# Linear attention in a decoder kernel: two row groups and two heads per unit, value blocks as stationary operand

## The reference, cut to what matters

```python
def _L2_attn_ref(x, W_qkv, W_out):
    nH, Hs = (16, 8)
    qkv = (x @ W_qkv.T).reshape(Bx, Tx, 3 * nH, Hs).transpose(0, 2, 1, 3)
    q, k, v = (qkv[:, :nH], qkv[:, nH:2 * nH], qkv[:, 2 * nH:])
    q = jax.nn.softmax(q, axis=-1) * Hs ** (-0.5)
    k_exp = jnp.exp(k - jnp.max(k, axis=2, keepdims=True))
    k_exp_cumsum = jnp.cumsum(k_exp, axis=2)
    kv_cumsum = jnp.cumsum(jnp.einsum('bhtc,bhtd->bhtcd', k_exp, v), axis=2)
    kv = kv_cumsum / (k_exp_cumsum[..., None] + 1e-09)
    xo = jnp.einsum('bhtc,bhtcd->bhtd', q, kv)
    return xo.transpose(0, 2, 1, 3).reshape(Bx, Tx, Dm) @ W_out.T
x = _layernorm(x + _L2_attn_ref(x, L2_attn_W_qkv, L2_attn_W_out), axis=-1)
```

## Time and profile before

| | us |
|---|---|
| median of 3 runs | 2258.78 (2258.63 to 2259.35) |
| profiled execution, its own time | 2261.14 |
| its span, first to last instruction | 2259.4 |
| mean granted TensorE clock in the span | 0.841 of 2.4 GHz |
| TensorE busy (matmul) | 1642.3, 73% |
| VectorE busy | 1300.3, 58% |
| ScalarE busy | 739.4, 33% |
| GpSimd busy | 385.6, 17% |

### The profile page before, as it was taken

The page is one execution under the profiler, slowest core; times in us unless marked ns, Lnnn a source line. Parts: engine busy times, 40 slices in busy tenths (PEclk is TensorE's granted clock), DMA queues, the critical chain, the costliest instruction groups (busy, mean ns, idle before and its releaser), DMA issues. The chain is left out here.

```text
span 2259.4 us, 25576 instructions
## 1 busy us (share of the span) xinstructions
PE 1642.3 (73%) x9160; PEld 1227.4 (54%) x9160; DVE 1300.3 (58%) x2377; ACT 739.4 (33%) x1362; POOL 385.6 (17%) x411
## 2 busy tenths in 40 slices
PE   3788888896759969994735984966835674876595
PEld 2466666675537656662524973655523662653373
DVE  4699999993755551114566546335245936733853
ACT  1456565651214423321211331012303223333242
POOL 0565655551000000000100000000001005001300
PEclk7799999997869989996767996967967976788597
DMA  5011111101000001000001210000010000000000
GB/s 171 26 34 34 35 34 35 34 13 48 1 0 1 1 0 53 31 10 0 1 0 67 101 56 0 1 1 0 1 75 1 1 1 0 1 1 1 0 1 10
DMA packets 21244, 49.79 MB, mean 22 GB/s; under 512 B 4752, under 2 KB 9232, under 8 KB 20880
## 3 DMA queue, kind: packets, MB, share of 16 engines
q1 hardware_dynamic: 21136, 48.40, 6.4%
HBM read 47.29 MB, written 1.10 MB: 21 GB/s over the span
## 5 line engine op out<-in xcount | busy, mean ns | idle before, releaser
L186 POOL TENSOR_TENSOR rstd<-spread,minus_half 128x4 f32<-128x4 f32 x36 | 36.7, 1020 | 1460.9 <-DVE spread L168 1460.9
L906 PE MATMUL l0h_scores<-l0h_k_rot,l0h_q_slots 128*128 128x128 f32 (+1 forms) x1024 | 206.9, 349 | 0.0
L906 PEld LDWEIGHTS l0h_scores<-l0h_k_rot,l0h_q_slots 128*128 128x128 f32 x1024 | 170.0, 208 | 13.1
L1110 POOL TENSOR_TENSOR l0h_k_part<-large_weights,l0h_sines 128x512 f32<-128x512 f32 x64 | 83.2, 1299 | 219.8 <-PE l0h_scores L906 127.1
L986 ACT ACTIVATE l0h_scores<-l0h_scores,l0h_top 128x128 f32<-128x128 f32 (+1 forms) x256 | 100.4, 392 | 26.1 <-DVE l0h_top L1063 26.0
L1485 DVE TENSOR_TENSOR l0e_weighted<-l0e_out_ps,l0f_weight 128x512 f32<-128x512 f32 x18 | 12.5, 692 | 151.0 <-PE l0e_out_ps L1447 151.0
L882 PE MATMUL l0h_projected<-XT,l0h_wq 128*128 128x256 f32 x256 | 71.0, 401 | 18.9 <-DVE l0h_q_rot L1050 9.8
L1467 ACT ACTIVATE l0e_hidden<-l0e_hidden_ps,l0e_experts 128x512 f32<-128x512 f32 x72 | 49.5, 687 | 107.2 <-PE l0e_hidden_ps L1433 107.2
L1444 PE MATMUL l0e_out_ps<-l0e_experts,l0e_hidden 128*128 128x128 f32 x576 | 82.5, 286 | 0.0
L1057 DVE TENSOR_TENSOR l0h_q_slots<-l0h_q_rot,l0h_chosen 128x1024 f32<-128x1024 f32 x64 | 78.4, 1225 | 7.0 <-DVE l0h_q_rot L1054 0.5
L1111 POOL TENSOR_TENSOR l0h_k_rot<-large_weights,l0h_cosines 128x512 f32<-128x512 f32 x64 | 81.9, 1280 | 0.0
(11 more groups left out here) (682 smaller groups left out, 4057.3 us busy)
## 6 DMA issues: line engine op xcount, KB each, us to landing
l1e_experts<-in_l_experts SPq DMA_DIRECT2D x16, 768.0 KB, 4.2
l0h_chosen<-l0h_chosen_dram SPq DMA_DIRECT2D x64, 128.0 KB, 2.9
l0e_experts<-in_l_experts SPq DMA_DIRECT2D x9, 578.0 KB, 3.8
l0h_pos<-l0h_pos_dram SPq DMA_DIRECT2D x64, 64.0 KB, 2.0
small_weights<-in_w_l_ffn SPq DMA_DIRECT2D x1, 4016.0 KB, 13.4
large_weights<-in_w_l_xattn SPq DMA_DIRECT2D x1, 2632.0 KB, 9.2
l0h_wq<-in_l_wq SPq DMA_DIRECT2D x16, 128.0 KB, 2.9
large_weights<-in_w_l_attn SPq DMA_DIRECT2D x2, 512.0 KB, 6.6
```

Of the source, the lines that this page charges most:

```text
L906: mm = nc.tensor.matmul(at[:, slot], q_slots[:, s % 2, slot, part, i * P:(i + 1) * P], k_rot[:, s % 2, part, 0:KEYS[i][1]], start=False, s ...
L1110: nc.gpsimd.tensor_tensor(k_part[:], source, at_batch(sines, s), ALU.mult)
```

## The change

- `flat` gets a block of 32 columns for each tile and head: 24 zeros and then the head's 8 values, and 24 zeros at the very end (4120 columns). The values are copied with gaps, and GpSimd clears 128 runs of 24 columns.
- A unit is now (b, p, jj): the row groups p and p + 2 and the heads 2jj and 2jj + 1 of each. `weigh` has four matmuls with 32 rows and 256 columns, which alternate between the two row groups; the two groups write to different PSUM banks.
- In the products the masked block is the moving operand and 32 columns of `flat` are the stationary one. The window is shifted by 8 columns for each head, so the four heads of a group fill the 32 output partitions 32g to 32g + 31 and are added in PSUM with zeros elsewhere. The result is already turned: features by partitions, tokens by columns.
- The cross part is one matmul for each batch with `state` as stationary operand (L1954 of the new kernel), added to the second tile's columns of the same PSUM bank. The cross product, its copy and the block with the addition are gone.
- ScalarE copies 256 columns for each batch, four times, and `close_sublayer` is called with `features_t`.

```diff
-        flat, values = padded_values(k, "l2a_values", T, HX, DX, ctx)
-        values = values.rearrange("p t h d -> p t (h d)")
-        running, queries, heads_out = sb("running", [P, N]), sb("queries", [P, 4, N]), sb("heads_out", [P, T, P])
+        flat = sb("values", [P, T * HX * 32 + 24])
+        blocks = flat[:, 0:T * HX * 32].rearrange("p (t h e) -> p t h e", t=T, h=HX)
+        values = blocks[:, :, :, 24:32]
+        running, queries, heads_t = sb("running", [P, N]), sb("queries", [P, 4, N]), sb("heads_t", [P, N])
...
-             lambda act, out: nc.scalar.copy(flat[:, 0:N], out)),
+             lambda act, out: nc.scalar.copy(values.rearrange("p t h d -> p (t h) d"),
+                                             out.rearrange("p (a d) -> p a d", d=DX))),
...
-                    nc.gpsimd.memset(flat[:, N:], 0.0)
+                    nc.gpsimd.memset(blocks[:, :, :, 0:24], 0.0)
+                    nc.gpsimd.memset(flat[:, T * HX * 32:], 0.0)
...
-            weights_ps = k.ps("l2a_weights_ps", [P, 2, TB, 4, P], inner)
+            weights_ps = k.ps("l2a_weights_ps", [P, 2, 2, TB, 2, P], inner)
...
-            units = [(b, g) for b in range(B) for g in range(4)]
+            units = [(b, p, jj) for b in range(B) for p in range(2) for jj in range(2)]
...
-                            mm = nc.tensor.matmul(weights_ps[:, n % 2, i], k_t[rows, tile], queries[rows, :, tile],
-                                                  start=True, stop=True)
+                            for o in range(2):
+                                rows = slice(32 * (p + 2 * o), 32 * (p + 2 * o) + 32)
+                                mm = nc.tensor.matmul(weights_ps[:, n % 2, o, i], k_t[rows, tile],
+                                                      queries[rows, 2 * jj:2 * jj + 2, tile], start=True, stop=True)
...
+                        for y in range(2):
+                            j = 2 * jj + y
+                            for i in range(TB):
+                                for o in range(2):
+                                    g = p + 2 * o
+                                    at = ((TB * b + i) * HX + 4 * g + j) * 32 + 24 - 8 * j
+                                    mm = nc.tensor.matmul(out_ps[32 * g:32 * g + 32, b % 2, i * P:(i + 1) * P],
+                                                          flat[:, at:at + 32], weights[:, n % 2, o, i, y, :],
+                                                          start=(j == 0 and i == 0), stop=False, skip_group_check=True)
+                        mm.then_inc(unit_ready, 1)
+                        if n % per_batch == per_batch - 1:
+                            nc.tensor.matmul(out_ps[:, b % 2, P:2 * P], state[:, b, :], q_t[:, b * S + P:(b + 1) * S],
+                                             start=False, stop=True, skip_group_check=True).then_inc(out_ready, 1)
...
-                        for i in range(TB):
-                            for j in range(4):
-                                mm = nc.tensor.matmul(out_ps[:, n % 2, (i * 4 + j) * DX:(i * 4 + j) * DX + P],
-                                                      weights[:, n % 2, i, j, :],
-                                                      flat[:, ((TB * b + i) * HX + 4 * g + j) * DX:][:, 0:P],
-                                                      start=True, stop=True)
-                        mm.then_inc(out_ready, 1)
...
-                second = heads_out[:].rearrange("p (b i) n -> p b i n", i=TB)[:, :, TB - 1, :]
-                nc.vector.tensor_tensor(second, second, cross[:], ALU.add)
-        close_sublayer(k, "l2a_close", heads_out[:], [W("wout")], 1)
+        close_sublayer(k, "l2a_close", None, [W("wout")], 1, features_t=[heads_t[:]])
...
-                pe.wait_ge(state_ready, 1)
-                for b in range(B):
-                    mm = nc.tensor.matmul(cross_ps[:, b, :], q_t[:, b * S + P:(b + 1) * S], state[:, b, :], start=True,
-                                          stop=True)
-                mm.then_inc(cross_ready, 1)
```

More of the change, by code:

```diff
@@ L1921, in weigh @@
                     def weigh(n):
-                        b, g = units[n]
-                        rows = slice(32 * g, 32 * g + 32)
+                        b, p, jj = units[n]
                         if n >= 2:
@@ L1931, in weigh, with product @@
                         mm.then_inc(ready, 1)
+                    def product(n):
+                        b, p, jj = units[n]
+                        pe.wait_ge(masked, n + 1)
+                        if n % per_batch == 0 and b >= 2:
+                            pe.wait_ge(out_used, b - 1)
+                        for y in range(2):
[11 more added lines that the diff above has]
+                                             start=False, stop=True, skip_group_check=True).then_inc(out_ready, 1)
@@ L1952, in _, with l2_attn_state @@
                         if n >= 2:
-                            v.wait_ge(out_ready, n - 1)
-                        nc.vector.tensor_tensor(weights[:, n % 2].rearrange("p i j t -> p (i j) t"),
-                                                weights_ps[:, n % 2].rearrange("p i j t -> p (i j) t"),
-                                                bc(seen[:].unsqueeze(1), [P, TB * 4, P]), ALU.mult).then_inc(masked, 1)
+                            v.wait_ge(unit_ready, n - 1)
+                        nc.vector.tensor_tensor(flat_unit(weights, n), flat_unit(weights_ps, n),
+                                                bc(seen[:].unsqueeze(1), [P, 4 * TB, P]), ALU.mult).then_inc(masked, 1)
                 @block.scalar
                 def _(act):
-                    for n, (b, g) in enumerate(units):
-                        act.wait_ge(out_ready, n + 1)
-                        nc.scalar.copy(heads_out[:, TB * b:TB * b + TB, 32 * g:32 * g + 32],
-                                       out_of(n).rearrange("p (i c) -> p i c", i=TB)).then_inc(out_used, 1)
-        with nc.Block() as block:
-            @block.vector
-            def _(v):
-                second = heads_out[:].rearrange("p (b i) n -> p b i n", i=TB)[:, :, TB - 1, :]
-                nc.vector.tensor_tensor(second, second, cross[:], ALU.add)
-        close_sublayer(k, "l2a_close", heads_out[:], [W("wout")], 1)
-def l2_attn_cross(k, k_t, q_t, values, cross):
+                    for b in range(B):
+                        act.wait_ge(out_ready, b + 1)
+                        nc.scalar.copy(heads_t[:, b * S:(b + 1) * S], out_ps[:, b % 2, 0:S]).then_inc(out_used, 1)
+        close_sublayer(k, "l2a_close", None, [W("wout")], 1, features_t=[heads_t[:]])
+def l2_attn_state(k, k_t, values, state):
     assert TB == 2
@@ L1978, in l2_attn_cross @@
     with ExitStack() as ctx:
-        rows_ps, state_ps, cross_ps = (k.ps("l2c_" + x, [P, B, P], ctx) for x in ("rows_ps", "state_ps", "cross_ps"))
-        rows, state = (k.sb("l2c_" + x, [P, B, P], F32, ctx) for x in ("rows", "state"))
-        turned, rows_ready, products_ready, state_ready, cross_ready = k.sems(
-            "l2c", "turned rows_ready products_ready state_ready cross_ready")
+        rows_ps, state_ps = (k.ps("l2c_" + x, [P, B, P], ctx) for x in ("rows_ps", "state_ps"))
+        rows = k.sb("l2c_rows", [P, B, P], F32, ctx)
+        turned, rows_ready, products_ready = k.sems("l2c", "turned rows_ready products_ready")
         with nc.Block() as block:
@@ L1991, in _ @@
                 for b in range(B):
-                    mm = nc.tensor.matmul(state_ps[:, b, :], rows[:, b, :], values[:, TB * b, :], start=True, stop=True)
+                    mm = nc.tensor.matmul(state_ps[:, b, :], rows[:, b, :], values[:, TB * b], start=True, stop=True)
                 mm.then_inc(products_ready, 1)
-                pe.wait_ge(state_ready, 1)
-                for b in range(B):
-                    mm = nc.tensor.matmul(cross_ps[:, b, :], q_t[:, b * S + P:(b + 1) * S], state[:, b, :], start=True,
-                                          stop=True)
-                mm.then_inc(cross_ready, 1)
             @block.scalar
@@ L2003, in _ @@
                 nc.scalar.copy(rows[:], rows_ps[:]).then_inc(rows_ready, 1)
-                act.wait_ge(cross_ready, 1)
-                nc.scalar.copy(cross[:], cross_ps[:])
             @block.vector
@@ L2010, in _ @@
                 for b in range(B):
-                    last = nc.vector.tensor_tensor(state[:, b, :].rearrange("p (h d) -> p h d", h=HX),
-                                                   state_ps[:, b, :].rearrange("p (h d) -> p h d", h=HX),
-                                                   bc(k.own_head.unsqueeze(2), [P, HX, DX]), ALU.mult)
-                last.then_inc(state_ready, 1)
+                    nc.vector.tensor_tensor(state[:, b, :].rearrange("p (h d) -> p h d", h=HX),
+                                            state_ps[:, b, :].rearrange("p (h d) -> p h d", h=HX),
+                                            bc(k.own_head.unsqueeze(2), [P, HX, DX]), ALU.mult)
 L2X = Pack("l2_xattn")
```

17 lines of the change are left out of this document (8 added, 9 removed).

## The result

The changed kernel takes 2253.26 us (median of 10 runs, 2251.26 to 2255.45) against 2259.07 for ten runs of the kernel before: a ratio of 0.9974, interval 0.9964 to 0.9984. Forecast was 2228.7 with a range of 2225 to 2243, so the change won a fifth of what I had expected, and the time lies outside the range. The profiled execution took 2253.92 us, its span is 2252.2.

The account below looks back on a forecast made before the run. TensorE's beat of 3.89 us a unit was taken to bound the unit loop, VectorE hidden. A gain of 31.1 us to the second addition, less 1.0 for the clearing, made 30.1: 2228.7 from 2258.78, range 2225 to 2243.

Parts of the forecast that it names:

- Part 3: Unit loop as a whole: 2.24 us a unit, VectorE hidden, full clock after unit 0, loop from 1410.70 to 1450.3.
- the release: TensorE's clock rising from 1.2 to 2.4 GHz, put at the end of unit 0 in the loop.
- Rival C: Unit loop: clock stays at 1.2 GHz because half-filled matmuls leave the array too idle; 4.1 us a unit, 2257; chance 0.03.
- Loop's start: Between state masking and unit loop: cross product and copy gone, loop begins at 1410.70, 0.30 us of barrier behind the masking.
- Unit 0: First unit of the loop, at 1.2 GHz: sums start 3.6 us after the loop's start and take 1.75.
- Part 1: Key-query products in the unit loop: two row groups overlap, 1.06 us a unit instead of 1.91.
- Part 2: Sums in the unit loop: two column groups overlap, 1.18 us a unit, bounds 1.04 and 1.98.
- Rival A: Sums in the unit loop: column groups do not overlap, staying at 1.98 us a unit; +13.6, 2242.3; chance 0.17.
- Rival B: Sums in the unit loop: each record waits for the one before, 4.6 us a unit, 2280; chance 0.03.
- The loop from start to last copy: Unit loop from its start at 1410.70, end of matmuls at 1450.3, then ScalarE's copy of 0.37 us.
- The close: After the loop: begins at 1451.0, 16 records take 2.02 us, second half added at 1453.0 instead of 1484.14.
- Part 5: Before the loop: larger clearing of 2.6 us holds VectorE's subtraction, +1.0 us, bounds 0 and +2; strided copy counted at nothing.

Follow-up runs that it names:

- weigh_first: The changed kernel with the second unit's key-query products issued five times over, 20 pairs of 32-row matmuls without interruption: 2259.77 us, ratio 1.0000.
- sums_first: The changed kernel with the first unit's sums issued four times over, 64 matmuls with 32-column blocks instead of 16: 2232.59 us, ratio 0.9879.
- prewarm: The changed kernel with six full-size matmuls of 512 columns, results not used, ahead of the first unit: 2232.85 us, ratio 0.9880.
- rows_only: The kernel before with only the key-query half changed to paired 32-row matmuls; sums, cross part and close as before: 2249.34 us, ratio 0.9960.
- serial: The changed kernel with one row group a unit, 512-column key-query products, and all sums of a unit into one group of 32 partitions: 2266.59 us, ratio 1.0031.
- bridged: The changed kernel with unused full-size matmuls where TensorE waits: thirteen of 512 columns in the softmax block, two more in the state block: 2225.20 us, ratio 0.9845.
- hidden: The changed kernel with eleven unused full-size matmuls of 512 columns in the softmax block, where TensorE waits for VectorE: 2253.50 us, ratio 0.9976.
- cols_full: The changed kernel with each key-query product over all 128 rows instead of its 32, so heads are not separated: 2242.14 us, ratio 0.9919.
- four_first: The changed kernel with forty unused 32-row matmuls of 256 columns, going round all four row groups, ahead of the first unit: 2235.76 us, ratio 0.9891.

## Why the prediction was wrong

**The step that failed** is in Part 3: "Here TensorE runs without a gap from 1410.70, so I put the release at the end of unit 0; three us of error either way are worth 1.5." The release did not come before 1473, at the very end of the loop. Rival C describes what happened (2257 forecast, 2253.3 measured; a beat of 4.1 forecast, 3.87 measured), and I gave it 0.03. Its reason, that half-filled matmuls leave the array too idle, fits the runs but is not shown by them.

Two readings led there. I took "TensorE busy" for the condition: weigh_first was busy without a gap at 0.50. And both rows cited against C were of other work. The projection with 32 columns has 32-column loads over all 128 rows, and in sums_first the clock rises in such work. It is no witness for 32-row products in two groups. The 64-row stream stood at 1.00 already when the row cited began, and prewarm shows that holding and gaining are two things. Its first run of 256 columns in that sublayer says more: the eight records that start at 1942.55 begin at 0.50, and the clock rises while they run (the stretch ahead, 1936.00 to 1942.55, is all at 0.50). They follow 1.9 us of full-height matmuls, so which of the two it answered can't be told.

```profile
1942.55:1944.16 1.61, 1.61 (x10) 1.11 (x9) 0.00 (x0) 0.37 (x1) 0.00 (x0) 0.65 0.00 0
```

But two groups of 64 rows take all 128 rows, as four groups of 32 do, and two groups of 32 take half. The kernel before had shown the gap in the evidence: its clock rose only at 1421.40, in the first full-size sums, after 3.79 us of pairs in units 0 and 1 at 0.50. I explained that with the idle time between them. rows_only has no such idle time, and its clock, too, rose only at 1421, 8 us after the loop's start; in weigh_first, with pairs alone, it didn't rise at all.

The sum, step by step, against the second addition (1453.0 + 1.0 forecast, 1477.19 measured, 23.2 later):

- Loop's start: 0.30 behind the masking forecast, 0.31 measured. Right.
- Unit 0: sums 3.6 after the loop's start forecast, 3.71 measured; their length at 1.2 GHz 1.75 forecast, 1.85 measured. Nearly right: the 3.37 us that I halved were not all at 1.2 GHz, since the clock rose at 1421.40 and they end at 1421.88. All at 0.50 they take 3.71 (rows_only, 1416.78 to 1420.49), and half of that is 1.86. Half of 3.37 would be 1.69, not 1.75.
- Part 1, key-query half: 1.06 forecast, 1.06 at the full clock (rows_only, prewarm), 2.01 at half.
- Part 2, sums: 1.18 forecast, 1.00 at the full clock (prewarm). The mechanism was right, the term 0.18 too dear. Rival A, 1.98, is refuted. Two column groups side by side take about half of what serial needs for the same columns (its sums are 1.86 us at the full clock, 1443.88 to 1445.74). The rule of the Trainium skill (TensorE: Matmul & The Clock Gate, Part 3), that a weight load overlaps running matmuls only if the row group differs, gave A's time; the 1.00 us for 16 loads and 16 matmuls in one row range disagrees with it.
- Rival B, sums waiting for each other in the same 32 partitions: 0.12 us a record at 1.2 GHz where it asked for 0.275. Refuted.
- The loop from start to last copy: 39.6 forecast, 63.28 measured. This is +23.6, the whole miss. With the clock at 1.00 from its start it takes 35.47 (prewarm).
- The close: 2.7 forecast from the copy to the second addition, 2.74 measured.
- Part 5: the clearing takes 2.66 us (2.6 forecast), but VectorE's subtraction beside it takes 1.23 (rows above), as without it: it wasn't held, and the 1.0 us charged isn't there. That term was wrong, and small. That this execution arrived 0.45 later has to do with no step of mine.

Had the clock been there, the change would have come out on the forecast's side: prewarm's second addition stands at 1454.00 although its loop starts at 1415.79, 5.1 later than I had it, and bridged ends at 2225.2.

## What to carry to other kernels

Halving the streaming by small tiles is worth nothing if TensorE stays at 1.2 GHz for it (a beat of 3.87 us for 3.89 here): before packing matmuls into two of four row groups, ask what in the program will raise the clock ahead of them and whether a gap can drop it. A row that shows packed matmuls at 1.00 shows that they hold the clock; only a stretch that begins at 0.50 shows what gains it. Where an engine ahead of such a loop waits anyway, full-height filler up to the loop's first instruction can be worth much (28 us between the changed kernel and bridged), while filler with TensorE idle behind it (2.76 and 0.68 us in hidden) was worth nothing. When a filled and an unfilled kernel are compared, compare the sublayer too and not only the whole: the rest of this program alone differs by up to 6 us between profiled executions (771.2 to 776.9).

## What the hardware showed beyond that

- Gaining and holding differ. The same loop stays at 0.50 for 60 us when it starts there and at 1.00 for 35 us when it starts there.
- What TensorE was doing when the clock rose: full-height products (cols_full, prewarm), 32-column blocks over 128 rows in a run of 5.44 us (sums_first), 32-row products over all four row groups (four_first). The same products in two row groups left it at 0.50 for 10.61 us (weigh_first). The changed kernel's own clock rose at 1473, where the sums of the last two units follow one another (32 records in 2.89 us from 1471.10). What in these runs makes the difference, and why serial got it only at 1442, stays open.
- A switch between 32-row and full-height matmuls costs 0.2 us at 2.4 GHz in the new loop, too (1.06 for 8 records that stream 0.107 each, 0.86), and 0.3 at 1.2 GHz (2.01 for 1.71). It is paid once a run and not once a record: weigh_first's 48 records leave the same 0.30 over (10.54 from their start to the sums, for 10.24). And it isn't tied to the rows: in cols_full both kinds take all 128 rows and only the width of the stationary operand changes, and 0.22 is left over (1.93 for 1.71).
- GpSimd's clearing of 2.66 us did not hold VectorE's operation with two operands in SBUF beside it, though one of another kind seems to have been held elsewhere in this program (3.75 us, where the next one on as many elements takes 0.43). Why the two differ was not tried.
